# Keys placed by strided transfers and routing work in other slots in the third attention, and the fourth attention's TensorE program written out, in an eight-part transformer kernel

## The reference, cut to what matters

```python
x = x + _L2_xattn_ref(_layernorm(x), ctx_1024, ctx_1024, mask, W_q, b_q, W_k, b_k, W_v, b_v, W_o, b_o)
x = x + _L2_ffn_ref(_layernorm(x), wg, w1, b1, w2, b2)
x = x + _L3_xattn_ref(_layernorm(x), ctx_1024, ctx_1024, Wq, Wk, Wv, Wo)
...
# in _L2_xattn_ref
scores = jnp.einsum('bhqd,bhkd->bhqk', Q, K) / math.sqrt(D_K)
scores = jnp.where(mask == 0, jnp.float32(-1000000000.0), scores)
attn = jax.nn.softmax(scores, axis=-1)
...
# in _L2_ffn_ref: 2 of 8 experts for each token, each expert with room for cap tokens
logits = xt.astype(jnp.float32) @ wg.astype(jnp.float32)
gvals, gidx = jax.lax.top_k(jax.nn.softmax(logits, axis=-1), K)
loc = jnp.cumsum(m, axis=0) - 1 + offset[None, :]
keep = pos < cap
disp = jnp.zeros((E, cap, D), x.dtype).at[e_flat, p_flat].add(x_rep * kmask[:, None])
```

## Time and profile before

| | us |
|---|---|
| time before, median of 3 runs | 4132.62 |
| lowest and highest run | 4130.66, 4158.82 |
| the profiled execution's own time | 4131.01 |
| its span | 4128.9 |
| TensorE matmuls busy in the span | 3458.1 (84%) |
| VectorE busy | 3417.6 (83%) |
| ScalarE busy | 2382.1 (58%) |
| GpSimd busy | 1545.5 (37%) |

### The profile page before, as it was taken

The page is one execution under the profiler, slowest core; times in us unless marked ns, Lnnn a source line. Parts: engine busy times, 40 slices in busy tenths (PEclk is TensorE's granted clock), DMA queues, the critical chain, the costliest instruction groups (busy, mean ns, idle before and its releaser), DMA issues. The chain is left out here.

```text
span 4128.9 us, 95016 instructions
## 1 busy us (share of the span) xinstructions
PE 3458.1 (84%) x31907; PEld 2505.8 (61%) x31907; DVE 3417.6 (83%) x6484; ACT 2382.1 (58%) x4440; POOL 1545.5 (37%) x935
## 2 busy tenths in 40 slices
PE   6983979998599788888568839989499998899999
PEld 3553647766477465565456627667366666677777
DVE  7888879999799788878755579889788888788888
ACT  2431657776277466655545527667576665466665
POOL 1210035553000345555444435545155563122222
PEclk9985989999599899989788969999699998899999
DMA  2001322222100222222121142222222222000000
GB/s 65 14 25 64 130 50 64 66 61 53 42 1 0 50 56 55 60 56 56 52 76 57 58 127 64 59 60 58 64 58 48 53 57 77 24 16 15 15 10 16
DMA packets 161066, 209.96 MB, mean 51 GB/s; under 512 B 38044, under 2 KB 110048, under 8 KB 157857
## 3 DMA queue, kind: packets, MB, share of 16 engines
q1 hardware_dynamic: 151457, 187.83, 16.8%
q0 software_dynamic: 8192, 16.92, 1.2%
q10 hardware_dynamic: 1152, 1.57, 0.2%
HBM read 53.09 MB, written 42.21 MB: 23 GB/s over the span
## 5 line engine op out<-in xcount | busy, mean ns | idle before, releaser
L1102 ACT ACTIVATE a_p<-a_p 128x480 f32<-128x480 f32 x832 | 501.7, 603 | 528.5 <-DVE a_p L939 521.8
L698 POOL TENSOR_TENSOR a_km<-a_k,a_slots 96x1920 fp32r<-96x1920 f32 x186 | 631.3, 3410 | 184.9 <-DMA a_k<-a_kh 181.2
L934 DVE TENSOR_REDUCE a_mx<-a_sc 128x4 f32<-128x480 f32 (+1 forms) x832 | 540.6, 650 | 129.8 <-PE a_sc L1206 106.4
L939 DVE TENSOR_TENSOR a_p<-a_sc,a_mx 128x480 f32<-128x480 f32 x832 | 531.8, 639 | 19.7 <-DVE a_mx L934 0.5
L1108 ACT ACTIVATE a_pt<-a_tp 120x512 f32<-120x512 f32 x832 | 485.4, 584 | 104.0 <-PE a_tp L1215 101.6
L1215 PE MATMUL a_tp<-ident,a_p 128*120 128x128 f32 x3328 | 518.9, 280 | 6.1 <-ACT a_pt L1108 6.1
L1200 PE MATMUL a_sc<-a_km,a_qr 96*128 96x480 f32 x768 | 403.5, 525 | 103.0 <-DVE a_p L939 71.5
L1215 PEld LDWEIGHTS a_tp<-ident,a_p 128*120 128x120 f32 x3328 | 414.7, 141 | 84.8 <-issue 37.2
L1239 PE MATMUL a_nd<-a_pt,a_vm 120*32 120x128 f32 x6656 | 297.6, 285 | 19.2 <-ACT a_pt L1108 18.8
L1200 PEld LDWEIGHTS a_sc<-a_km,a_qr 96*128 96x128 f32 x768 | 149.0, 194 | 210.4 <-issue 116.6
L2196 ACT ACTIVATE f_s<-f_pu 128x512 f32<-128x512 f32 x256 | 153.5, 600 | 212.4 <-PE f_pv L1678 212.4
(11 more groups left out here) (455 smaller groups left out, 8840.3 us busy)
## 6 DMA issues: line engine op xcount, KB each, us to landing
a_qr<-a_qh SPq DMA_DIRECT2D x372, 64.0 KB, 2.0
a_k<-a_kh SPq DMA_DIRECT2D x384, 60.0 KB, 2.0
a_ctx<-in_ctxT SPq DMA_DIRECT2D x64, 240.0 KB, 2.7
a_qr<-a_ql SPq DMA_DIRECT2D x186, 64.0 KB, 2.0
a_k<-a_kl SPq DMA_DIRECT2D x192, 60.0 KB, 2.0
dispatched<-f_empty SPq DMA_DIRECT2D x8, 1040.0 KB, 20.9
f_xr<-dispatched SPq DMA_DIRECT2D x32, 260.0 KB, 2.6
chosen<-f_none SPq DMA_DIRECT2D x8, 1024.0 KB, 11.8
```

Source lines behind the costliest of these rows:

```text
L698: v.tensor_tensor(KM[par][:, i, :, :].rearrange("p b (j k) -> p b j k", k=KN), K3[:, i, :, :].unsqueeze(2).to_broadcast([TR, GB, 4, KN]), ...
L934: v.tensor_reduce(mx[:], view, AX.X, ALU.max).then_inc(mx_ready, 1)
L939: v.tensor_tensor(PR[s % 4][:].rearrange("p (h k) -> p h k", k=k), view, mx[:].unsqueeze(2).to_broadcast([P, heads, k]), ALU.subtract).the ...
L1102: a.activation(PR[s % 4][:], PR[s % 4][:], ACT.Exp).then_inc(exp_ready, 1)
```

## The change: what it does, and the diff

It touches four things.

1. In a2, from the second group on, the masked keys are no longer multiplied by GpSimd. The columns of the key and query weights are put in another order inside each block of 32 (so that row 4r + j of a block is feature r of head j), SyncE stores the three terms in DRAM (`stacked_keys`, three DMAs) and four more DMAs, one for each head j, copy every fourth row of a_km's 96 from there into block j. The other rows of a_km stay zero: one buffer has its zeros from the first group, the other gets them from one memset of GpSimd.
2. To have that order, a2's key and query weights are first loaded into a_pt and copied by ScalarE (`reorder`), the two biases come in four DMAs each and the slot table in three, some of them issued by ScalarE.
3. The pieces of `Route` get other slots. ScalarE's writing of rt_hl moves from slots 7 and 9 to 5 and 12, its copies to 9, 11, 14 and 18; TensorE's turns from 9 and 11 to 10 and 15, its router matmuls from 10 and 12 to 12 and 19 (19 is slot 3 of the next group); VectorE's choice of experts from slot 13 to slot 4 of the next group, and what follows it moves back too. GpSimd's scatters are split 7 and 3 for a group instead of 3, 2, 2 and 3.
4. a3's TensorE program is written out for all 16 groups instead of a loop.

```diff
@@ Route.vector @@
             for n in range(4):
-                yield
+                if n % 2 == 1:
+                    yield
...
-            yield from self.at("dve", self.GROUPS * b + 3, 13)
+            yield from self.at("dve", self.GROUPS * b + 4, 4)
             dve.wait_ge(self.l_ready, self.GROUPS * (b + 1))
...
-            yield from self.at("dve", self.GROUPS * b + 4, 4)
+            yield from self.at("dve", self.GROUPS * b + 4, 9)
             dve.wait_ge(self.ex_ready, b + 1)
...
-            yield from self.at("dve", self.GROUPS * b + 4, 6)
+            yield from self.at("dve", self.GROUPS * b + 4, 10)
...
@@ Route.tensor @@
-                yield from self.at("pe", self.GROUPS * b + 3, 9 + 2 * i)
+                yield from self.at("pe", self.GROUPS * b + 3, 10 + 5 * i)
...
-                yield
+                self.held = (self.hs_ready, g + 1)
+                yield from self.at("pe", self.GROUPS * b + 3, 12 + 7 * i)
                 pe.wait_ge(self.hs_ready, g + 1)
+                self.take_bank(pe)
+                self.after_main(pe)
...
-            yield from self.at("pe", self.GROUPS * b + 4, 5)
+            yield from self.at("pe", self.GROUPS * b + 4, 10)
...
@@ attention_phase, SyncE @@
+                def place_keys(g, par):
+
+                    sp.wait_ge(low_ready["k"], g + 1)
+                    for term, part in enumerate((HIGH, LOW, HIGH)):
+                        kept = R.keys.rearrange("(t q i f) -> t i q f", t=3, q=32, i=4)[term]
+                        sp.dma_start(kept, part["k"][:].bitcast(F32)).then_inc(keys_kept, 16)
+                    sp.wait_ge(keys_kept, 48 * g)
+                    if par == 1:
+                        sp.wait_ge(keys_empty, 1)
+                    at_least(sp, sc_ready, (g - 1) * S)
+                    of_head = R.keys.rearrange("(q j s k) -> j q s k", q=24, j=4, k=KN)
+                    for j in range(4):
+                        sp.dma_start(KM[par][j:TR:4, :, :, j * KN:(j + 1) * KN].bitcast(F32),
+                                     of_head[j]).then_inc(keys_in, 16)
...
@@ attention_phase, GpSimd @@
                 def prepare(g, par):
                     low_part("k", g)
-                    masked_keys(pool, nc.gpsimd, g, par, (0,))
-                    scatter(g - 1, 4, 3)
+                    if not route:
+                        masked_keys(pool, nc.gpsimd, g, par, (0,))
+                    scatter(g - 1, 4, 7)
                     low_part("q", g)
-                    masked_keys(pool, nc.gpsimd, g, par, (1,))
-                    scatter(g - 1, 11, 2)
-                    masked_keys(pool, nc.gpsimd, g, par, (2,))
-                    scatter(g - 1, 13, 2)
-                    masked_keys(pool, nc.gpsimd, g, par, (3,))
+                    if not route:
+                        masked_keys(pool, nc.gpsimd, g, par, (1, 2, 3))
                     scatter(g - 1, 15, 3)
...
+                    nc.gpsimd.memset(KM[1][:].bitcast(F32), 0.0).then_inc(keys_empty, 1)
...
@@ attention_phase, ScalarE @@
+                if route:
+                    dims_first(act, 1, bk, keys_first_in)
+                    by_dim = I["slots"].rearrange("(t j r) w -> t r j w", t=3, j=4)
+                    for term in range(3):
+                        act.dma_start(slots[32 * term:32 * term + 32, :], by_dim[term]).then_inc(keys_first_in, 16)
...
@@ attention_phase, TensorE @@
                     if packed and j == 0:
-                        pe.wait_ge(km_ready[i], g + 1)
+                        if not route or g == 0:
+                            pe.wait_ge(km_ready[i], g + 1)
+                        elif i == 0:
+                            pe.wait_ge(keys_in, 64 * g)
...
-                if own_keys or route:
+                if own_keys or route or causal is not None:
                     groups_in_full(group)
```

90 lines of the change are left out of this document (68 added, 22 removed).

## The result

The changed kernel takes 4094.49 us, the median of 4 runs (4090.51 to 4097.86). The kernel before takes 4138.43 us in the same comparison (4 runs, 4130.66 to 4158.82). The ratio is 0.9888, with a 95% interval of 0.9855 to 0.9921. So the change gains 1.1%, half of what was forecast (4044), and the time lies just above the range. The profiled execution took 4094.84 us, its span is 4093.0.

The account below looks back on a forecast made before the run. Bound in a2 by VectorE's routing work, GpSimd's holds on it and idling, in a3 by issue gaps. -66 + 2 - 5 - 19 = -88 from 4131.0 gives 4043, with 1.6 for the median 4044; range 4008 to 4094.

Parts of the forecast that it names:

- GpSimd's multiplications go: In a2's groups 3 to 13, removing GpSimd's key masking ends most of its 45 us hold on VectorE: gain 43 us.
- rival 4: In a2's groups 1 to 15 the keys come late at slot 0 and the kernel gets slower, up to 4329 us; chance 0.04.
- The prediction's own signs: Wrong if TensorE waits for a_km's transfers, VectorE idles 6 us or more per a2 group, or 5 us gaps remain in a3.
- Groups 3 to 13: Stretch of a2 with routing, 456.0 us before: gain 66 us, 43 from the holds and 23 from the slots.
- The slots: In a2's groups 3 to 13 the routing's new slots remove 17.7 us of waits and 5 of other idling: gain 23 us.
- The new path of the keys: In a2, three stores and four transfers replace 12 copies, start about 8 us into the group and cost nothing; cover 12 us.
- Start of a2: Extra issue ahead of the mask and the memset of a_km at a2's start: +2 us, between 0 and +5.
- Groups 14 and 15 and the head of f2: End of a2 and start of f2: groups 9 us less, head about 4 more; sum -5, between -10 and +4.
- a3 written out: In a3, gaps from the loop's jump back go: gain 19 us, bounds 0 and 21.
- number 1: In a2, VectorE and TensorE interlock better and idling sinks by 51 instead of 23 us: 4016 us; chance 0.13.
- number 3: a3's longer program shifts later code, so 5 us gaps appear in the loop of s3 or f3: 4061 us; chance 0.07.
- Number 2: Only a2's holds go; waits return in other slots and a3's gaps stay: 4087 us; chance 0.14.

## Why the prediction was wrong, step by step

**The step that failed** is in "GpSimd's multiplications go": it said that GpSimd "is not on the path itself", and counted only what its multiplications held. They did a second thing. They stood between the scatters and kept them in twos and threes. With them gone the scatters come in bursts of up to five, and TensorE's signals come late and its instructions one by one. It is the multiplications' going and not the new slots: with the old slots the bursts cost 455.5 - 414.1 = 41 us as well, and beside the multiplications spacing took 0.4 us off with the new slots and 10 or 21 with the old, by which of the two profiles of the old program is taken. No rival had this either, though rival 4 looked for a transfer that hurts. The cost is 427.0 - 387.9 = 39 us, and 66 - 39 = 27 is what was measured (29). In the profile before nothing could point at it, since that execution has next to no late signals; the scatters' spacing was in the order of GpSimd's instructions. The prediction's own signs told of the failure: VectorE idled 81 / 11 = 7.4 us a group in the profile after, where 6 or more was to mean that it was wrong, and the clock was 0.94 and not above 0.95. Its bounds, added up, reached 4099; the range was cut at 4094, and the time lies between.

**Groups 3 to 13, the rest.** With the scatters spaced the stretch went down by 57.6 us (445.5 to 387.9), or 68.1 from the 456.0 of the profile shown; forecast 66. The sum came near, but in part by luck, as its terms depend on each other. VectorE's work fell by 37.7 us where 43 were forecast (the sentence on the Trainium skill's rule had 38), and the stretch by 31.4 us for the key path alone. The slots, forecast at 23, are worth 26 beside the new keys, and the wait for rt_hl went as said. That the two parts are independent was an unspoken step, and it is false: forecast for the slots alone would have been -23, measured +18. Of the Trainium skill's rule ("SBUF — State Buffer", "Who interferes with whom") that the remaining low parts still hold VectorE one row shows the effect: L338 keeps its 1193 ns, five times, each ending with a low part of the keys, 5 us in all.

**The new path of the keys** cost nothing, as forecast, but for a weaker reason. The stores did not land in 2.0 us but in 10: the transfers of a_km are issued 15.2 us into the group (1664.29 - 1649.10), and not 8. Seven of the 12 us of cover were used up, and TensorE never waited for keys, not even in groups of 28.4 us. The rows for 2.0 us were copies of 32 partitions, 60 KB each; the stores are of 128 partitions in an order whose slowest dimension is 4, and stores of 32 rows each again land within 2 us. The Trainium skill has that rule ("DMA: Bandwidth & Descriptors", "Why a DMA increments its semaphore by 16 and not by 1"): a transfer uses as many of the 16 engines as divide the slowest dimension of both sides. By it the stores use four. The trace agrees: its DMA records have 12 packets of 4 B beside the three stores, four for each, and in the run with twelve stores of 32 rows 192, that is 16 for each.

**Start of a2**: +6.8 against +2 (0 to +5). The sum "the memset replaces no more than the multiplications took" overlooked that it too holds VectorE, at a place where VectorE had work. That is the longer first group; the other 3.5 us are the later first key copy. The run with the early memset still had 3.0 of them and made them up in the first group.

**Groups 14 and 15 and the head of f2**: -5 forecast, +7.0 seen. Most of it is the two groups, 82.7 us against 77.2, where 9 less were forecast; the head is 2.6 us longer, where 4 were. But the old program gave 485.7 us for the whole in the run with a3's line, and 485.5 with its scatters spaced, with 87.1 and 86.2 us for the two groups. The 478.9 of the profile before was the low end. So the term is about 0 as far as these profiles tell, mis-sized by 5. The scatters have a part here too: without them the two groups take 71.4 us.

**a3 written out**: -22.7 against -19 (0 to -21); all gaps are gone and every group but the first two takes 27.9 us. The line alone gives this, and against the other profiles of the loop 28 to 32.

Of the rivals, number 1 (4016), number 3 (gaps behind a3, where the profile after has 2 us more in all) and number 4 (late keys) did not occur. Number 2 came near in time (4087) for reasons that are wrong: the waits did not come back in other slots, and a3's gaps went.
